# One kernel, a mixture of experts between two attentions: the down-projection split into float32r products, one ring for all expert weights, and two weight transposes moved

## The reference, cut to what matters

```python
h = jax.nn.silu(jnp.einsum('nf,efh->enh', x, w1)) * jnp.einsum('nf,efh->enh', x, w3)
y = jnp.einsum('enh,ehf->enf', h, w2)
out = jnp.einsum('enf,ne->nf', y, full_w)     # full_w: two nonzero weights per row
```

```python
h = silu(bit_linear(x, w_gate)) * bit_linear(x, w_up)    # bit_linear: x rounded to 8 bits, w to -1, 0, 1
return bit_linear(rms_norm(h, ln_weight), w_down)
```

## Time and profile before

| what | us |
|---|---|
| median of 3 runs | 1581.54 |
| lowest, highest | 1578.25, 1591.35 |
| the profiled execution | 1582.63 |
| its span, first to last instruction | 1580.7 |
| TensorE, VectorE, ScalarE, GpSimd busy | 1310.6, 1212.1, 997.3, 335.0 |

### The profile page before, as it was taken

The page is one execution under the profiler, slowest core; times in us unless marked ns, Lnnn a source line. Parts: engine busy times, 40 slices in busy tenths (PEclk is TensorE's granted clock), DMA queues, the critical chain, the costliest instruction groups (busy, mean ns, idle before and its releaser), DMA issues.

```text
span 1580.7 us, 24025 instructions
## 1 busy us (share of the span) xinstructions
PE 1310.6 (83%) x8549; PEld 768.5 (49%) x8596; DVE 1212.1 (77%) x1799; ACT 997.3 (63%) x1291; POOL 335.0 (21%) x317
## 2 busy tenths in 40 slices
PE   8992888888865799999999997655777777779886
PEld 3441455555534566666666664313343444444333
DVE  6998899999976655555666664876999999984963
ACT  5775788888853455544455551335889888882574
POOL 1113200000004444445552004001112111110440
PEclk9996999999987899999999999766888778779998
DMA  8996455445344899999999975399887789783001
GB/s 293 288 288 164 94 114 133 121 117 122 79 167 190 327 416 417 414 417 418 415 415 403 354 273 173 65 204 212 174 170 171 162 164 177 164 145 96 1 1 53
DMA packets 453868, 338.65 MB, mean 214 GB/s; under 512 B 367464, under 2 KB 369512, under 8 KB 453136
## 3 DMA queue, kind: packets, MB, share of 16 engines
q1 hardware_dynamic: 439488, 291.31, 63.6%
q0 software_dynamic: 9920, 37.75, 6.3%
q10 hardware_dynamic: 4368, 8.39, 1.4%
HBM read 205.86 MB, written 38.01 MB: 154 GB/s over the span
## 4 chain that ended last, share of the span: by engine, by line
PE 37%; DVE 29%; issue 16%; DMA 7%; ACT 5%; POOL 3%; SPq 2%; POOLq 0%; DVEq 0%; ACTq 0%
DVE arena L2066 12%; PE scores L1137 8%; DMA arena<-in_L_ffn_w 5%; PE bank L1169 4%; PE scores L1236 4%; PE bank L1019 4%; PE scores L1003 2%; DVE arena L1836 2%; PE bank L1283 2%; DVE arena L1822 2%; PE scores L1002 2%; ACT arena L1480 2%; PE scores L1265 1%; PE bank L1381 1%; POOL xs_d L861 1%
## 5 line engine op out<-in xcount | busy, mean ns | idle before, releaser
L2066 DVE TENSOR_SCALAR_CACHE_REDUCE arena<-scores,arena 128x1024 f32<-128x1024 f32 x256 | 314.4, 1279 | 45.2 <-PE scores L1236 44.3
L1920 DVE TENSOR_TENSOR wlo<-raw,whi 128x2048 fp32r<-128x2048 f32 x92 | 219.8, 2409 | 157.8 <-ACT whi L1531 157.8
L1610 ACT ACTIVATE arena<-arena 128x2048 int16<-128x2048 f32 x128 | 273.5, 2149 | 74.9 <-POOL arena L902 39.3
L1236 PE MATMUL scores<-arena 96*128 96x512 bf16 x512 | 193.3, 485 | 85.3 <-DVE arena L2066 77.9
L1531 ACT ACTIVATE whi<-raw 128x2048 fp32r<-128x2048 f32 x92 | 173.2, 1908 | 51.1 <-PE scores L1137 51.1
L1169 PE MATMUL bank<-arena 128*128 128x512 f32 x368 | 163.8, 594 | 4.0 <-DMA arena<-in_L_ffn_w 3.9
L1137 PE MATMUL scores<-whi,xhi 128*128 128x512 f32 x368 | 159.3, 433 | 3.8 <-DVE xlo L1924 2.1
L1137 PE MATMUL scores<-whi,xlo 128*128 128x512 f32 x368 | 146.3, 398 | 0.0
L1137 PE MATMUL scores<-wlo,xhi 128*128 128x512 f32 x368 | 146.2, 397 | 0.0
L1480 ACT ACTIVATE arena<-scores 128x512 f32<-128x512 f32 (+3 forms) x256 | 116.6, 506 | 26.2 <-PE scores L1003 26.2
L1822 DVE TENSOR_REDUCE arena<-scores 128x1 f32<-128x640 f32 (+3 forms) x128 | 127.6, 1018 | 4.8 <-PE scores L980 4.4
(11 more groups left out here) (292 smaller groups left out, 2336.3 us busy)
## 6 DMA issues: line engine op xcount, KB each, us to landing
raw<-in_L_ffn_w SPq DMA_DIRECT2D x92, 1024.0 KB, 13.2
arena<-in_L_ffn_w SPq DMA_DIRECT2D x46, 1024.0 KB, 18.4
arena<-arena SPq DMA_DIRECT2D x32, 256.0 KB, 2.9
kst_d<-arena POOLq DMA_DIRECT2D x16, 384.0 KB, 5.6
tern_d<-arena POOLq DMA_DIRECT2D x12, 512.0 KB, 6.8
arena<-kst_d SPq DMA_DIRECT2D x16, 384.0 KB, 4.0
xs_d<-arena SPq DMA_DIRECT2D x23, 256.0 KB, 2.9
arena<-xs_d SPq DMA_DIRECT2D x22, 256.0 KB, 16.4
```

What stands on the lines that cost most here:

```text
L1236: ins = pe.matmul(scores[:, s:s + 512], qhead[h % 2][0:K3, t * P:(t + 1) * P], khead[h % 2][0:K3, s:s + 512], start=True, stop=True)
L1610: act.activation(dst, src, ACT.Exp, bias=ebias[n % SBUFS], scale=-1.0, accum_out=rsum[h % 2][:, t:t + 1]).then_inc(p_ready, 1)
L1920: dve.tensor_tensor(wlo[:, n % SPLITS], raw[:, n % RAWS], whi[:, n % SPLITS].bitcast(F32), ALU.subtract).then_inc(lo_done, 1)
L2066: dve.tensor_scalar(ssb[i][:, s:s + 1024], scores[:, s:s + 1024], nsq[:, h, t:t + 1], None, ALU.mult, ALU.min, accum_out=nmx[i][:, half:ha ...
```

## The change: what it does

The down-projection takes the same form as the up-projections. ScalarE rounds both halves of the turned hidden rows (hhi), VectorE subtracts (hlo), and TensorE makes hhi*whi + hhi*wlo + hlo*whi for each of the eight chunks. The halves of w2 are pieces like the others: they go through raw, whi and wlo. So a slot has six pieces; all are counted in one order, piece_of(u, i), which is the order in which TensorE uses them; the first piece of a slot comes ahead of the w2 halves of the slot before. RAWS goes from 6 to 7, SPLITS from 3 to 4, and the three wdown buffers go. One semaphore half_used takes the place of up_done and down_done. The router's scratch tensors move to other places, so SP no longer waits for the turned rows before the second slot's first piece; it asks for piece (0,5) and for slot 1's pieces 1 to 3 later, the latter behind the scatter.

The two transposes of tern_d leave their place: w_gate's goes out once the last slot's hidden rows are turned, w_up's behind the first two heads' keys. For that the output buffers yb move out of the region of wT[0].

```diff
-PIECES = 4 * SLOTS
-RAWS, SPLITS, DOWNS = 6, 3, 3
+PIECES = 6 * SLOTS
+RAWS, SPLITS = 7, 4
...
+def piece_of(u, i):
+
+    if i == 0:
+        return max(6 * u - 2, 0)
+    if i < 4:
+        return 6 * u + i
+    return 6 * u + i + (1 if u + 1 < SLOTS else 0)
...
+            load_piece(1, 0, chosen[1])
+            sp.wait_ge(r_step, R_LAST)
+            load_piece(0, 5, 0)
+            sp.wait_ge(scattered, 16 * 2 * NT)
+            sp.dma_start(xsin[1], xs_d[P:2 * P, :]).then_inc(xs_loaded[1], 16)
+            for u in range(1, SLOTS):
+                if u + 1 < SLOTS:
+                    load_rows(u + 1)
+                for i in range(1, 4):
+                    load_piece(u, i, chosen[u])
+                if u + 1 < SLOTS:
+                    choose(u + 1)
+                    load_piece(u + 1, 0, chosen[u + 1])
+                for i in range(4, 6):
+                    load_piece(u, i, chosen[u])
...
+            sp.wait_ge(h_turned, 2 * SLOTS)
+            turn_weights(0)
...
             load_keys(0)
             load_keys(1)
+            turn_weights(1)
...
-            for w in range(2):
-                sp.dma_start_transpose(wT[w].rearrange("p o c n -> p (o c) n"), tern_d[w]).then_inc(wT_in, 16)
...
             def down(u):
-                for half, ready in enumerate((hT0_ready, hT1_ready)):
-                    m = 2 * u + half
-                    pe.wait_ge(down_in[m % DOWNS], 16 * (m // DOWNS + 1))
-                    pe.wait_ge(ready, u + 1)
+                for half in range(2):
+                    s = piece_of(u, 4 + half)
+                    pe.wait_ge(lo_done, s + 1)
+                    pe.wait_ge(hlo_ready, 2 * u + half + 1)
                     if half == 0 and u:
                         pe.wait_ge(y_ready, u)
-                    for c in range(4 * half, 4 * half + 4):
-                        ins = pe.matmul(bank7[:, :], hT[:, c], wdown[m % DOWNS][:, c % 4], start=c == 0, stop=c == EC - 1)
-                    ins.then_inc(down_done, 1)
+                    for c in range(4):
+                        for h, w in ((hhi, whi), (hhi, wlo), (hlo, whi)):
+                            ins = pe.matmul(bank7[:, :], h[:, 4 * half + c], w[:, s % SPLITS, c // 2, c % 2 * 512:c % 2 * 512 + 512],
+                                            start=half == 0 and c == 0 and h is hhi and w is whi, stop=half == 1 and c == 3 and h is hlo)
+                        if c % 2:
+                            ins.then_inc(half_used, 1)
```

ScalarE's slot, and then VectorE's, as they are after the change (the lines that are taken out are left out here):

```diff
             def slot(u):
                 more = u + 1 < SLOTS
+                round_piece(6 * u + 4)
+                round_piece(6 * u + 5)
+                silu(u, 0)
                 if more:
...
                     round_slot(u + 1)
...
+                silu(u, 1)
+                round_piece(6 * u + 6)
+                round_piece(6 * u + 7)
+                if u:
+                    act.wait_ge(half_used, 2 * piece_of(u - 1, 5) + 2)
+                round_h(u, 0, bank4)
+                round_h(u, 1, bank5)
+                round_piece(6 * u + 8)
+                round_piece(6 * u + 9)
                 if u >= 2:
                     act.wait_ge(y_stored[u % 2], 16 * (u // 2))
...
             def slot(u):
...
+                rest_of_piece(6 * u + 4)
+                rest_of_piece(6 * u + 5)
+                if u + 1 < SLOTS:
                     rest_of_slot(u + 1)
...
+                gate(u, 0)
+                gate(u, 1)
+                rest_of_piece(6 * u + 6)
+                rest_of_h(u, 0, bank4)
+                rest_of_h(u, 1, bank5)
+                rest_of_piece(6 * u + 7)
+                rest_of_piece(6 * u + 8)
+                rest_of_piece(6 * u + 9)
```

More of the change, by code:

```diff
@@ L314, in program @@
         assert rm.at <= oatt_at + 4 * GT * D
-        over_xn = Region(m_mark, WT_AT)
+        over_xn = Region(m_mark, WT_AT - 2 * 4 * D)
         wchunk_late = over_xn.take(F32, TERN_COLS)
         tern_late = over_xn.take(BF16, TERN_COLS)
-        rs = Region(WT_AT)
+        rs = Region(WT_AT - 2 * 4 * D)
+        yb = [rs.take(F32, D) for _ in range(2)]
         xsin = [rs.take(F32, D) for _ in range(2)]
@@ L325, in program @@
         sg = rs.take(F32, EH)
-        hT = rs.take(F32, EC, P)
-        yb = [rs.take(F32, D) for _ in range(2)]
+        hhi = placed(F32R, "hhi", rs.at, EC, P)
+        rs.at += 4 * EH
+        hlo = placed(F32R, "hlo", rs.at, EC, P)
+        rs.at += 4 * EH
         posi = rs.take(I32, 2, NT)
@@ L334, in program @@
         wm, posm, posl = ([rs.take(F32, NT) for _ in range(2)] for _ in range(3))
[L336 to L340, removed]
-        lgT = over_lo.take(F32, T)
[L342 to L348, removed]
+        XT = Region(whi_at + 2 * 4 * PIECE, wlo_at).take(F32, KC, T)
+        over_lo = Region(wlo_at + 2 * 4 * PIECE, m_mark)
+        oh0, ohl, ohl2 = (over_lo.take(F32, NT, P) for _ in range(3))
+        lgT = over_lo.take(F32, T)
+        over_raw = Region(raw_at + (RAWS - 1) * 4 * PIECE, whi_at)
+        gwT = over_raw.take(F32, KC, E)
+        r8 = [over_raw.take(F32, NT, E) for _ in range(12)]
+        asg = over_raw.take(BF16, NT, E)
+        te = [over_raw.take(F32, E) for _ in range(6)]
+        cmp = over_raw.take(F32, SLOTS + 1, E)
+        slot_f = over_raw.take(F32, SLOTS + 1)
         gath = Region(raw_at, whi_at)
@@ L638, in _ @@
             sp.wait_ge(att_added, 1)
-            for n in range(4):
-                load_piece(n, 0)
-            for m in range(2):
-                load_down(m, 0)
+            for i in range(5):
+                load_piece(0, i, 0)
             sp.wait_ge(r_step, R_SLOTS)
@@ L1973, in _, with rest_of_h, gate @@
             assert n == R_LAST
+            def rest_of_h(u, half, bank):
+                cols = slice(4 * half, 4 * half + 4)
+                dve.wait_ge(hhi_ready, 2 * u + half + 1)
+                dve.tensor_tensor(hlo[:, cols].rearrange("p c n -> p (c n)"), bank[:, :],
+                                  hhi[:, cols].rearrange("p c n -> p (c n)").bitcast(F32), ALU.subtract).then_inc(hlo_ready, 1)
+            def gate(u, half):
+                cols = slice(half * 512, half * 512 + 512)
+                dve.wait_ge(silu_done, 2 * u + half + 1)
+                dve.wait_ge(half_used, 2 * piece_of(u, 3) + half + 1)
+                dve.tensor_tensor(sg[:, cols], scores[:, 1024 + half * 512:1536 + half * 512], sg[:, cols], ALU.mult).then_inc(h_done, 1)
             def slot(u):
[L1976 to L1978 removed]
+                rest_of_piece(6 * u + 4)
+                rest_of_piece(6 * u + 5)
+                if u + 1 < SLOTS:
                     rest_of_slot(u + 1)
[L1980 to L1991 removed]
+                gate(u, 0)
[6 more added lines that the diff above has]
+                rest_of_piece(6 * u + 9)
             rest_of_slot(0)
```

161 lines of the change are left out of this document (57 added, 104 removed).

## The result

| | before | after |
|---|---|---|
| median, us | 1584.12 of 4 runs | 1602.07 of 4 runs |
| lowest, highest | 1578.25, 1591.35 | 1599.54, 1606.90 |
| the profiled execution | 1582.63 | 1599.54 |
| its span | 1580.7 | 1597.8 |
| mean granted clock | 0.903 | 0.897 |

(The median of before has moved from 1581.54 by one more run.) The ratio is 1.0129, with a 95% interval of 1.0108 to 1.0150. So the changed kernel is 1.3% slower, less than 2% but clear of the noise. The forecast was 1557, with a range up to 1577, so it was wrong in sign.

The account below looks back on a forecast made before the run. Transfers were taken to bound slots beside GpSimd, TensorE those after, with a queue-order stall after the last query tile. Slots 7 + stall 19 - 1 = 25 us off 1582.6 gave 1557.6, stated as 1557; range 1540 to 1577.

Parts of the forecast that it names:

- The down-projection on TensorE: Expert slots: 24 products at 0.232 us, 5.57 us, replace 6.87 us; 1.3 us less per slot on TensorE.
- the layout of ScalarE's and VectorE's work: Within a slot: splitting fits, VectorE 16.2 of 18.0 us; about 0.3 us lost, 18.35 us per slot, TensorE the bound.
- VectorE against GpSimd: Slots beside GpSimd: shared-port exclusion costs between nothing and 5.7 us a slot; taken as 0 to 0.4, hidden beside transfers.
- near end: Low side of the lock cost: GpSimd's operations fall in VectorE's free time of 3.9 us, 0 to 0.4 us a slot.
- Rival (c): Slots beside GpSimd: full lock, 5.7 us on each, 22.3 us a slot; 34 us lost against 18 gained, 1599; chance 0.05.
- The value part: Slots while GpSimd makes the values: 20.2 us each, as now, rather than the 18.7 that transfers would allow.
- Rival (e): Slots: TensorE's granted clock falls to 0.5 after longer waits, up to 2 us a slot; up to +15, 1570; chance 0.07.
- The ring of 7: Weight buffers: same 6.82 MB a slot; down(0) still ends at 541 us, then transfers set 20.1 us a slot beside GpSimd.
- (b): Slots beside GpSimd: partial lock, 21 us for 16 slots; 13 us lost against 18 gained, 1577; chance 0.11.
- The moved transposes: After the last query tile: stall shortened, 19 us gained; 0 charged beside the gathers, 1 us lost behind the first keys.
- (a): Slots: lock costs nothing, transfers and TensorE alone set the pace, value part 18.7 us a slot; 1545 to 1540; chance 0.20.

Follow-up runs that it names:

- no_loads: split_spread with GpSimd held to one chunk per slot and all its loads but the first left out; 1582.22 us, one execution, beside 1579.87 for the kernel before.
- small_ops: split_spread with GpSimd held to one chunk per slot and most of its operations cut to few columns, transfers kept; 1568.41 us, one execution.
- before_small: spread_only with GpSimd held to one chunk per slot and its operations cut as in small_ops; 1564.41 us, ratio 0.9882.
- w0_only: Kernel before with only w_gate's transpose moved, to the end of the last slot; 1577.53 us, one execution, beside 1583.41 for the kernel before.
- moved_only: Kernel before with both weight transposes moved as in the change and nothing else; 1576.84 us, ratio 0.9960.
- split_spread: Changed kernel with the weight transposes cut into sixteen parts as in spread_only; 1600.41 us, ratio 1.0108.
- spread_only: Kernel before with its two weight transposes cut into sixteen parts, sent under the second attention ahead of tiles TensorE turns; 1566.98 us, ratio 0.9906.
- w1_only: Kernel before with only w_up's transpose moved, behind the first keys; 1575.92 us, one execution, beside 1583.41 for the kernel before.

## Why the prediction was wrong

The profiled execution was forecast at 1557.6 and took 1599.54, 42 us more: 29 by down(21), 6 up to the last addition, 3 in the scores (15.4 gained where the text had 18), and 4 at the end.

**The down-projection on TensorE: right.** TensorE's timeline after the change, an up-projection behind a wait and later the down-projection:

```profile
826.27 0.76 PE L1132 MATMUL scores<-whi,xhi 128*128 128x512 f32 x1 [5.39 <-DVE wlo L1928]
826.83 0.63 PE L1132 MATMUL scores<-wlo,xhi 128*128 128x512 f32 x1
827.26 0.63 PE L1132 MATMUL scores<-whi,xlo 128*128 128x512 f32 x1
827.68 0.63 PE L1132 MATMUL scores<-whi,xhi 128*128 128x512 f32 x1
...
832.49 0.40 PE L1165 MATMUL bank<-whi,hhi 128*128 128x512 f32 x1
...
835.04 0.39 PE L1165 MATMUL bank<-whi,hlo 128*128 128x512 f32 x1
```

The last two are the first and the twelfth of the new products: (835.04 - 832.49) / 11 = 0.232 us from one to the next, as the text had it. And the slots without GpSimd take 18.32 us for a forecast of 18.35. By that period the layout of ScalarE's and VectorE's work holds too.

**"VectorE against GpSimd", the lock cost taken "near end, 0 to 0.4 a slot": this step failed.** In `after`, from 560 to 860, the group of the subtraction stands so:

```profile
L1928 DVE TENSOR_TENSOR wlo<-raw,whi 128x2048 fp32r<-128x2048 f32 x84 | 248.9, 2994 | 9.5 <-ACT whi L1530 9.2
...
L834 POOL TENSOR_SCALAR arena<-arena 128x2048 f32<-128x2048 f32 x11 | 44.0, 3998 | 108.9 <-DMA arena<-in_L_ffn_w_up 41.7 <-DMA arena<-in_L_ffn_w_down 38.9 <-DMA arena<-in_L_ffn_w_gate 28.3
```

A subtraction takes 2.99 - 2.29 = 0.70 us more than its own length, times six a slot 4.2 us, and VectorE is busy 286.79 of the 300 us. The text set out the budget: 16.2 us of VectorE's own work and 5.7 of GpSimd's make 21.9 for a period of 20.1. The slots came out at 21.57 on average, though unevenly (18.3 to 26.2). What was wrong was the choice between the ends: I took the near one because "such an overlap happened to few of 87 subtractions so far". That count was made in a slot with 11.2 + 5.7 = 16.9 us of claims on 20.1, where GpSimd could find a hole; it says nothing about a slot with 21.9. The changed kernel shows what happens when there is no hole. VectorE and GpSimd in the value part:

```profile
832.14 18.66 DVE L1928 TENSOR_TENSOR wlo<-raw,whi 128x2048 fp32r<-128x2048 f32 x5
```

```profile
831.83 4.62 POOL L872 TENSOR_TENSOR arena<-arena 128x2048 f32<-128x2048 f32 x1 [7.28 <-DMA arena<-v_d]
836.54 3.83 POOL L874 TENSOR_SCALAR arena<-arena 128x2048 f32<-128x2048 f32 x1
840.45 3.81 POOL L876 TENSOR_SCALAR arena<-arena 128x2048 bf16<-128x2048 f32 x1
```

Five subtractions take 18.66 us, where alone two take 4.49, so five 11.2. The other 7.5 us lie beside the three GpSimd operations. The timeline, asked for each of the five, gives 6.46 us for the first, which ends at 838.60, 2.15 behind L872, and 3.98 for the second. The second and third GpSimd operations, of a size that takes 1.90 us alone, show 3.8, as each waits for a subtraction. They alternate: one of one engine, one of the other. The Trainium skill (SBUF — State Buffer, "SBUF: two separate sides") gives the pair of ports to whichever of the two starts first, for the whole instruction. The trace agrees: the first subtraction needs another 2.15 us, about its whole own length, once L872 has ended.

**Rival (c)'s mechanism held; that its time came out is in part luck.** It had down(21) end at 990, a loss of 34 us, and the trace has 978.4, a loss of 22. The other 12 us came from what (c) did not have: 6.0 at the gathers, 15.4 gained in the scores where it had 18, and 4.3 at the end.

The value part was priced too low with the same reason ("20.2 us a slot, as now"): measured 21.0, 26.2, 25.7 and 22.6. There GpSimd stores nothing and waits 5.4 to 9.6 us for a chunk instead of 8.5 to 11.3, so its operations come closer together, and the three on a chunk take 12.7 us instead of 11.4. The slot of 26.2 falls in the window with the clock at 0.91. Rival (e) is in part true: in the timeline above TensorE's products come every 0.42 us instead of 0.23 after the wait of 5.39. It wasn't isolated. `no_loads` bounds it from one side: its clock is 0.99, and its slots are still held.

**"The ring of 7. It carries no fewer bytes": incomplete.** The bytes are the same, but fewer of them are moved ahead of slot 1, and the text gave this lead no price. With the lock off, `small_ops` ends down(21) at 952.3 where the text had 949. Of these 3 us a part is a miscount: the forecast has fifteen slots beside GpSimd and six behind it, where its own rivals (b) and (c) have sixteen and five, as the traces do, and that is 20.2 - 18.35 = 1.9 us. Against `before_small` the last slots are still faster (18.3 for 19.3 to 19.4), and down(21) ends no earlier; that the smaller lead took this gain away is argued, as said above.

**The moved transposes: the mechanism right, one cost missed; this step failed too.** The stall went from 21.19 us to 3.82, the scores gained 15.4 us of the 18 forecast, and behind the first keys the second transpose cost nothing. The step is "It runs beside the gathers; these are set by GpSimd's issue, so I cost it at 0 (up to 3 if a late gather is hit)". The gathers landed after 10.7 us instead of 3.6, and the additions came 6.0 us later in the changed kernel, 7.9 in `w0_only` and 8.7 in `moved_only`. The rows of before showed the room only in bandwidth; they did not show how gathers fare beside a transpose, and so 0 to 3 was a guess within a bound that no row carried.

**The end.** From the last score read to the last store the kernels need 157.9 us (before, `w0_only`) to 163.9 (`moved_only`, `split_spread`), without order by part of the change. The 4.3 us of this case lie within that scatter, and their cause stays open.

**The chances.** The forecast and (a), 0.70 together, rested on GpSimd still finding room, though the budget was over the period by 1.8 us with VectorE's operations on PSUM counted in. 0.05 for the case that it binds, beside 0.11 for (b), was the error of judgement.

## What to carry to other kernels

For two engines that exclude each other, add both engines' exclusive work and hold the sum against the period. Here 16.9 of 20.1 cost about 4 us in all and 21.9 of 20.1 cost 24.5, so that rare overlaps in a loop with room said nothing about one without. The sum is an estimate of the new period and no more: for 21.9 the slots took 20.2 (the ternary part of `no_loads`) to 21.6 us (all sixteen in the changed kernel). A long DMA transpose cost 6 to 10 us at two of the three places where it stood, ahead of the probability tiles and beside the gathers, and nothing that shows behind the first keys; cut into sixteen parts, each where SP had nothing else to send, it was hidden, and that alone (`spread_only`, 0.9906, 0.9881 to 0.9930) beat both kernels.

## What the runs showed of the hardware that was not expected

- A transpose of 2 MB from DRAM holds SP's queue for 8.0 to 10.2 us away from the gathers and for 24.2 to 28.1 us beside them, and it slows these: median time to landing 10.7 us in the changed kernel instead of 3.6. The windows from 960 to 1000 of `moved_only`, with such a transpose, and then of `w1_only`, without:

```profile
960.00:1000.00 40.00, 18.73 (x56) 9.44 (x54) 14.63 (x21) 3.24 (x5) 16.00 (x16) 0.80 0.87 168
```

```profile
960.00:1000.00 40.00, 19.52 (x60) 10.16 (x59) 22.16 (x40) 5.11 (x8) 16.74 (x16) 0.81 0.40 118
```

  The DMA engines are then busy at 0.87 for 168 GB/s, where weights reach 416 GB/s at 1.03. So in this stretch the GB/s alone would have told of room that the busy share does not show.
- VectorE's subtractions in a row don't keep GpSimd out, nor the reverse: with both ready they took turns, and a GpSimd operation of 1.90 us took 3.8.
